# Sixteen score products of a cross-attention step, spread over twelve slots by a table

## The reference

```
xq  = layernorm(result, ln2);  xs = layernorm(src, ln2)        # src: 8 x 750 x 512
k2, v2 = heads(split(xs @ ed_wkv));  q2 = heads(xq @ ed_wq)
wei2 = softmax(einsum('bhtd,bhjd->bhtj', q2, k2) * scale)       # 16 heads, 224 x 750 scores each
ed_out = merge(einsum('bhtj,bhjd->bhtd', wei2, v2)) @ ed_wproj + ed_bproj
```

## Time and profile before

| | us |
|---|---|
| median of 3 runs (1408.04 to 1412.78) | 1411.64 |
| the profiled execution | 1410.75 |
| its span, first to last instruction | 1408.9 |
| PE busy | 1331.1 (94%) |
| DVE busy | 828.3 (59%) |
| ACT busy | 667.1 (47%) |
| POOL busy | 655.3 (47%) |
| transfers, share of 16 DMA engines (data) | 49.7% |

### The profile page before, as it was taken

How to read it: one execution, slowest core, us unless ns; L and a number is a source line. 1 busy time by engine, 2 the same in 40 slices (tenths; PEclk the granted TensorE clock), 3 DMA queues, 4 the chain that set the end, 5 groups by cost and what they waited for, 6 DMA issues and landing times.

```text
span 1408.9 us, 26161 instructions
## 1 busy us (share of the span) xinstructions
PE 1331.1 (94%) x9705; PEld 1102.3 (78%) x9705; DVE 828.3 (59%) x2056; ACT 667.1 (47%) x1622; POOL 655.3 (47%) x547
## 2 busy tenths in 40 slices
PE   5799999999999999999689899999999999999998
PEld 5699899988878888888577777777877777787764
DVE  5412222225467687766745867677586767757565
ACT  4322122224556665656433556473564647456343
POOL 2233233323436555548733555555455455554451
PEclk9999999999999999999899999999999999999999
DMA  5411100123666554476268775576566567555641
GB/s 166 142 38 45 45 22 22 45 75 126 131 148 128 141 137 120 123 148 149 87 136 137 122 99 108 80 117 103 95 115 97 114 90 110 103 95 79 88 69 40
DMA packets 98257, 142.13 MB, mean 101 GB/s; under 512 B 9597, under 2 KB 62629, under 8 KB 98146
## 3 DMA queue, kind: packets, MB, share of 16 engines
q1 hardware_dynamic: 98146, 140.67, 49.7%
HBM read 59.40 MB, written 22.02 MB: 58 GB/s over the span
## 4 chain that ended last, share of the span: by engine, by line
PE 73%; DVE 6%; DMA 5%; POOL 5%; issue 5%; ACT 4%; SPq 1%; POOLq 0%; ACTq 0%; DVEq 0%
PE ps L179 20%; PE ps L1641 18%; PE ps L417 10%; PE ps_pair L1658 6%; PE ps L1673 6%; PE ps L1687 5%; PE ps L1741 4%; DVE ca_xT L1629 1%; DMA sa_K_stack<-sa_rows 1%; DVE ca_maxes L1576 1%; ACT ca_xT_f L1563 1%; POOL sa_rows L170 1%; POOL sa_rows L172 1%; POOL sa_fin L1001 1%; PE ps L1705 1%
## 5 line engine op out<-in xcount | busy, mean ns | idle before, releaser
L1507 POOL TENSOR_TENSOR ca_partial<-ca_partial,ca_probT 125x896 f32<-125x896 f32 x118 | 251.6, 2132 | 216.4 <-ACT ca_probT L1524 211.8
L1524 ACT ACTIVATE ca_probT<-ps_pair 125x448 f32<-125x448 f32 x384 | 210.4, 551 | 205.9 <-PE ps_pair L1658 204.6
L1576 DVE TENSOR_REDUCE ca_maxes<-ps 112x1 f32<-112x375 f32 x512 | 253.2, 539 | 83.7 <-PE ps L1673 83.2
L1673 PE MATMUL ps<-ca_k_stack,ca_q_stack 96*112 96x376 f32 x512 | 173.5, 369 | 17.3 <-DVE ca_maxes L1576 14.8
L1658 PEld LDWEIGHTS ps_pair<-ca_q_stack,ca_k_stack 98*125 98x125 f32 x768 | 130.6, 187 | 54.0 <-issue 40.7
L417 PE MATMUL ps<-ff_w,ff_hT 128*128 128x512 f32 x672 | 160.8, 396 | 6.4 <-DVE ff_w L63 6.4
L1658 PE MATMUL ps_pair<-ca_q_stack,ca_k_stack 98*125 98x224 f32 x768 | 163.2, 295 | 2.3 <-ACT ca_probT L1524 2.2
L301 POOL TENSOR_TENSOR ff_hT<-ff_hrelu,ff_hT 128x256 fp32r<-128x256 f32 x112 | 86.1, 771 | 162.5 <-DVE ff_hT L382 162.5
L1641 PE MATMUL ps<-ca_xT,w_a 128*128 128x376 f32 x768 | 155.9, 340 | 0.0
L1641 PE MATMUL ps<-w_b,ca_xT 128*125 128x512 f32 x576 | 151.4, 399 | 0.7 <-DVE sa_res L1128 0.5
L417 PEld LDWEIGHTS ps<-ff_w,ff_hT 128*128 128x128 f32 x672 | 126.1, 191 | 33.0 <-issue 4.2
(11 more groups left out here) (137 smaller groups left out, 2403.9 us busy)
## 6 DMA issues: line engine op xcount, KB each, us to landing
ca_k_stack<-ca_keys SPq DMA_DIRECT2D x96, 376.0 KB, 8.0
sa_Q_stack<-sa_rows SPq DMA_DIRECT2D x96, 112.0 KB, 3.7
sa_K_stack<-sa_rows SPq DMA_DIRECT2D x96, 112.0 KB, 3.9
ca_q_stack<-q_out SPq DMA_DIRECT2D x96, 112.0 KB, 9.8
ctx_tokens<-in_ctx_dram SPq DMA_DIRECT2D x14, 750.0 KB
ctx_tokens<-in_L_xattn_ff_w_dram SPq DMA_DIRECT2D x16, 512.0 KB, 4.7
q_out<-sa_yT SPq DMA_DIRECT2D x16, 448.0 KB, 4.0
ff_xin<-in_x_dram SPq DMA_DIRECT2D x7, 512.0 KB, 3.8
```

Source lines behind the costliest of these rows:

```text
L1507: pool.tensor_tensor(total, total, half(a), ALU.add).then_inc(partial_done, 1)
L1524: act.activation(probT[u // GH][0:JT, u % GH].rearrange("p a t -> p (a t)"), ps_p[u % 2][0:JT, 0:2 * T], ACT.Exp).then_inc(exp_done, 1)
L1576: dve.tensor_reduce(maxes[:, q, j, a:a + 1], ps_s[n % 3][0:TQ, 0:JH], AX_X, ALU.max).then_inc(s_read, 1)
L1673: pe.matmul(ps_s[n % 3][0:TQ, 0:JP], q_stack[0:KS, h, TQ * q:TQ * (q + 1)], k_stack[0:KS, h, a, :], start=True, stop=True).then_inc(s_psum, 1)
```

## The change

The sixteen scores of a step stood two in each of the slots 4 to 11. A table now gives, for each slot, the range of scores that it holds: one in slot 0, one in slot 1, none in slots 2 and 3, one in slot 4, one in slot 5, two in each of the slots 6 to 11. So score 0 moves from slot 4 to slot 0, score 1 from slot 4 to slot 1, score 2 from slot 5 to slot 4, and score 3 from the end of slot 5 to its beginning. The other twelve stay. M, in slot 2, comes behind scores 0 and 1 in the ring of three banks, where it came before them.

As the first score of all is now in slot 0 of step 1, the list behind it holds items that `EARLY` has placed already; they are left out there.

```
@@ plan_attention
-    return items + [("ca",) + o for o in other[start:]]
+    return items + [("ca",) + o for o in other[start:] if o not in early]
@@
 SLOTS = 12
+SCORED = (0, 1, 2, 2, 2, 3, 4, 6, 8, 10, 12, 14, 16)
@@ plan_cross_attention
         for i in range(SLOTS):
             scores = []
-            if 0 <= s - 1 < NG and 4 <= i:
-                scores = [("score", s - 1, 2 * (i - 4) + a) for a in range(2)]
+            if 0 <= s - 1 < NG:
+                scores = [("score", s - 1, u) for u in range(SCORED[i], SCORED[i + 1])]
```

## The result

| | median, us | ratio to the kernel before, 95% interval |
|---|---|---|
| before | 1412.21 | |
| changed | 1479.63 (1477.5 to 1481.67) | 1.0481 (1.0452 to 1.0511) |

The change costs 67 us, 4.8%. The forecast was 1471, 59 us over before; the time lies in the range.

What follows compares the result with a forecast made beforehand. PE, busy 94% of the span, was taken as the bound, with score 0 in slot 0 waiting for transfers. Terms 28 + 3.5 + 1.2 + 10.4 + 16 = 59 us on 1411.6 gave 1471 us, range 1446 to 1488.

Steps and rivals of the forecast that it cites:

- (a): Score 0 of groups 4, 8, ... 28 waits for the last key transfer: 4.0 us in seven places, 28 us.
- DVE's entry: Sign in the profile after: PE's score waits for DVE fall from 14.8 us to about 8.
- (b): Score 0 of groups with G % 4 = 2 waits for late queries: 0.4 to 0.6 us, seven times, 3.5 us.
- (c): Steps with s % 4 = 3: one more score delays ACT's copy of V, 0.17 us, seven times, 1.2 us.
- (d): Steps with s % 4 = 1: their keys and queries land before the next step begins, cost 0.
- (e): Query waits at steps 2, 3 and 32: 3.1, 4.6 and 2.7 us, together 10.4 us.
- (g): PE's clock falls to 1.2 GHz behind nine idles of 3 to 5 us: 1.8 us each, 16 us.
- The clock holds: Rival: all waits come but PE's clock stays full; 43 us slower, 1455 us, chance 0.25.
- Faster: Rival: transfers land earlier, so score 0 never waits for a landing; 4.7 us gained, 1407 us, chance 0.04.
- the clock holds and (a) is 1 us smaller each time: Case that set the lower end of the forecast range, given as 1446 us.
- The gain that spreading can give: PE's score waits for DVE, 14.8 us in 20 places, bound from above what spreading gives directly.

Runs made afterwards that it cites:

- no_landing: Changed kernel, but scores 0 and 1 read the stacks of the group before and the wait for transfers stands at score 2; 1408.3 us.
- two_transfers: Changed kernel, but only two of the three key transfers are sent for groups 4, 8, ... 28; 1440.6 us.
- clock_kept: Changed kernel, with 18 useless matmuls put in front of score 0 of groups 4, 8, ... 28; 1462.8 us.
- only_mod3: Kernel before, with the new table in steps with s % 4 = 3 alone; 1421.0 us.
- middle_even: Kernel before, but in even steps from 6 on one score stands in each of slots 2 to 5; 1401.4 us.
- middle_three: As middle_even, and in steps 7, 11, ... 27 two scores in each of slots 2 to 9, none in slot 10, two in slot 11; 1402.3 us.

## Why the prediction was right, point by point

**The mechanism** held in each part: the landing of keys and queries set the waits (no_landing, two_transfers), the ring and DVE's order did not, and the slowdown behind the waits was the clock (clock_kept). The time came 8 us above the forecast, and the lengths of the steps in the two traces tell where. Of the 7.5 us by which the profiled executions (1408.9 and 1475.7 us) differ more than the 59.3 of the sum, some 3 lie in the seven key waits, 3 in step 23 alone, 1.5 in the other steps with s % 4 = 3, 1 at step 32, and steps 2 to 4 were 1 us cheaper than in the sum.

**(a) Keys.** Listed at 29.0 us in seven places, where 28 us of delay stood in the sum. In step 16 to 17 score 0 went 1088.14 - 1063.20 = 24.9 us behind the start of step 16, where 1055.7 - 1031.07 = 24.6 was worked out. The difference is the ring and the transfer: score 0 of step 16 starts at 1063.90, 0.70 us behind its step and so 0.5 later than the 0.22 of a score that needn't wait, where 0.3 stood in the sum, and the last key transfer took 10.5 us, not 10.4. The same ring wait, 0.32 us of idle in front of score 0 in each of eight steps, is why DVE's entry fell to 10.7 us only, where about 8 was forecast. That the 0.65 us of idle of the earlier trace rows would be swallowed by the same landing held too; it is not in the list any more, and PE is idle for 4.37 us, with 4.5 named.

**(b) Queries.** Step 18 took 1130.91 - 1111.97 = 18.94 us in place of 19.27, and in step 19 score 0 came at 1131.97, 1.06 us behind the start:

```profile
1131.97 0.40 PE L1674 MATMUL ps<-ca_k_stack,ca_q_stack 96*112 96x376 f32 x1 [0.68 <-issue]
```

Less the 0.22 us that two prob matmuls take, 0.84 us of wait; less the 0.33 saved, 0.5, as in the sum. Step 19 is the cheapest of its kind, the others (step 23 apart) start score 0 about 1.15 us behind, 0.6 net.

**(c) ACT's start.** Step 15 took 1063.20 - 1041.20 = 22.00 us in place of 20.82. Its own score 0 came 1.17 us behind the start (1042.37 in the same timeline), 0.95 too late; what remains, 22.00 - 0.95 - 20.82 = 0.23, is the term for ACT, 0.17 in the sum; no_landing, where no query wait stands in the way, has 21.00 against 20.82, 0.18. That two maxima fewer on DVE give nothing there, only_mod3 showed.

**(d) Steps with s % 4 = 1** cost nothing but in step 5: the queries of group 5 landed late in the trace of before too, and step 6 waits 0.47 us for them, which the sum left out.

**(e) First and last steps.** Waits of 2.72, 4.75 and 2.64 us before score 0 of steps 2, 3 and 32 against 3.1, 4.6 and 2.7 in the sum. The first two are the "7.5, 2, 4.7" in the list of waits; behind all three the clock fell too, where the sum had it behind the first two.

**(g) The clock** is the term that was too small. The sum had 1.8 us for each of nine waits, 16 us, and by clock_kept the seven waits for keys cost 2.2 each, as much as its upper bound. What was mis-sized is the length of the low stretch. The sum took 5 us from one row and 3.9 from the stretch 745 to 750, but the clock was low ahead of that stretch already (trace of before):

```profile
740.00:745.00 5.00, 3.69 (x10) 2.40 (x11) 4.44 (x10) 0.85 (x2) 0.98 (x2) 0.71 0.70 154
```

0.71 over 5 us is 2.9 us at the low level, so with the 3.9 behind it this low stretch lasted 6.8 us. Behind the key waits of the changed kernel the low clock lasts from 3.2 us (step 9) to 6.3 (step 21), 33 us in the seven. Step 21, with a wait of 4.30 us, is the longest:

```profile
1177.70:1184.00 6.30, 6.30 (x22) 6.20 (x23) 2.35 (x5) 1.70 (x4) 0.00 (x0) 0.50 0.00 0
```

The sentence of the Trainium skill, page "TensorE: Matmul & The Clock Gate", section "HAM oscillation — how this bites in real kernels", that half of the throttled time is paid, gave an estimated 22 us for nine waits. The trace agrees with its half: 15.1 us lost of 33 us at the low level is 0.46. The factor 1.8 from the V matmuls gives 0.44, so the factor was right too.

Two more low stretches stand behind waits and were not priced in the sum. One follows the 2.64 us of idle in front of score 0 of step 32. The other stands in step 23, where the wait for queries lasted 2.2 us in place of 0.8, and the clock fell behind it. No run was made for it, but the traces point to a cause. The last query transfer of group 22 lands 10.8 us after its issue:

```profile
L1433 SPq DMA_DIRECT2D ca_q_stack<-q_out x3: 477/788/882, 1211.7 to 1213.4; - x3
...
DMA to landing us min/median/max: 9.9/10.2/10.8
```

In the ten traces kept there are 80 such transfers (the last of the queries sent in a step with s % 4 = 2). Seven took 10.7 to 10.8 us, the other 73 took 9.2 to 9.6. In the seven, and in no other, a transfer of the queue that the profile names "instruction" starts 2.7 to 2.9 us before the landing. In six others it starts some 1 us before, and they are not late. That the one causes the other is not shown by an experiment.

**The rivals.** "The clock holds" would have been 1455; it is what clock_kept comes near, 1462.8, with the clock held by force in seven of nine places. "Faster", with no wait for a landing, was put at 1407; no_landing measured 1408.3, of which some 3.8 us are the context transfer of its step 4. The point from which it decides, 3.5 us less of transfer, is nearly what two_transfers did: it takes away all but 1 us of each of these waits. One bound was worked out wrongly: "the clock holds and (a) is 1 us smaller each time" is 1455 - 7 = 1448 us, not 1446; nothing hangs on it.

**The gain that spreading can give** was bounded by the 14.8 us of the earlier trace rows; where it was taken without the waits (middle_even) it was 9 us.

## What to carry to other kernels

Before an instruction is moved forward in an in-order list, look up when each thing that it waits for arrives, its transfers above all, and in each kind of round: here two kinds of step had about 1 to 2 us in hand, one lacked a few tenths, and the fourth lacked 3.4 us (a landing at 1055.1 against a start at 1051.7). The wait itself is then only the first part of the price; everything behind it on the engine waits too, and here a PE that stood still for 4 us paid on average half as much again in clock. And a stretch that two engines pace together does not get shorter by relieving one of them: what DVE no longer held up in middle_three, ACT held up one slot later.

## What the runs showed of the hardware

- Idles of PE of about 1 us left the granted clock at 1.00 (two_transfers: 1.05 us, key half at 1.19 us). So did one of 2.02 us in clock_kept (step 7; 1.00 over the 3.9 us behind it), but behind one of 2.18 us in the changed kernel (step 23) the clock fell, as it did behind all those of 2.6 to 4.75 us. That 18 matmuls of no use in front of a wait save 2.2 us each time was not expected in that size.
- The three key transfers of a group with 376 KB each land one behind the other, 5.4, 8.0 and 10.4 us after issues 0.6 to 0.7 us apart. The last one of group 16 took 10.4 us before and 10.5 us after:

```profile
DMA to landing us min/median/max: 5.5/8.0/10.5
```

- Landings do not repeat whatever stands around them: the last key transfer of group 4 took 12.1 us before and 10.3 us after, and one query transfer in the changed kernel 10.8 us in place of 9.4.
